# Layer norm of the gathered features with rows on partitions, and the first block row used twice in the ramp: a two-layer graph kernel

## The chip, the cores and the metric

The kernel runs on one core of a Trainium2 chip. Its engines are named as in the profile: PE (TensorE, matmuls; PEld is its weight load), DVE (VectorE), ACT (ScalarE), POOL (GpSimd) and SP (SyncE, which only issues DMAs here). All arithmetic is float32. The metric is the device time of one execution in microseconds (us), less is better. Three runs of the kernel before gave 819.17, 820.83 and 821.37 us, median 820.83.

## The reference

With N = 4096 nodes, D = 128 features and a dense 4096 x 4096 matrix `adj` (64 MB), two layers are computed:

```python
h = relu(adj @ x @ gcn_w + gcn_b)
h = (h - h.mean(-1)) * rsqrt(h.var(-1) + 1e-5) * ln_g + ln_b
xz = h @ w_in                                # 128 -> 2 x 256: xc and z
u = silu(causal_conv4(xc) + conv_b)
dt, B, C = u @ w_xp                          # 8, 16 and 16 columns
dt = softplus(dt @ w_dt + b_dt)
state = exp(dt * A) * state + dt * B * u     # over 4096 steps, 256 x 16 states
y = (sum_s state * C + u * D_skip) * silu(z)
x1 = layernorm(x + y @ w_out)

out1 = MLP3(2 * (adj @ x1)); out2 = MLP3(2 * (adj @ x2))   # eps = 0
out = layernorm(x1 + [out1, out2] @ Wm.T + bm)
```

So `adj` is multiplied three times: with `x`, with `x2` (an input of its own), and with `x1`, which exists only as far as the scan over the nodes has come.

## The kernel before, in words

**Tiling.** `adj` is cut into 8 x 8 blocks of 512 x 512 (1 MB each). Block (n, m) adds, to row chunk n of a product, what the 512 nodes of column m give: 4 matmuls of 128x128 by 128x512 for each product. A block used for `x` and `x2` at once (`ONE`) or for `x2` and `x1` (`DOUBLE`) costs 8 matmuls and one load. `RING = 4` blocks lie in SBUF; SP loads the next one when one is used up. The `x` sums grow in PSUM bank `p_x`, the `x2` sums in `p_x2`; sums for `x1` are made in pieces (`SUMS`) in `p_two`, `p_x` or `p_x2` and added into `acc2` by DVE (`add_sum`, L958).

**Stages.** A *ramp* multiplies block row 0 by `x` (`RAMP`, 32 matmuls), then the chain of steps of chunk 0 runs with matmuls of row 1 between (`FILL`). Then come 8 *chunks* c = 0..7 of 16 *units* (one for each state s), then a tail with the last column of `x1` and the MLPs of layer 2. In unit s of chunk c DVE runs the scan over 512 nodes for the 2 x 128 channels (L933, twice), copies the last state (L941) and multiplies by C (L942); ACT makes exp(dt A) for the next unit into `p_dA` (L687); POOL makes dt B u two units ahead (`times_B`, `bh`, L1116) and adds the product into `y` (`add_product`, L1125). One unit has two *slots* on PE, so a chunk has 32.

**The chain.** Beside the units of chunk c the same engines prepare chunk c + 1 and finish c - 1. Preparing, on PE: `gcn` (L536), `cen` (L539, subtracts the mean by a matmul with a constant matrix), `var` (L542, averages the squares by another), `in_x` (L547, L552), `x_proj` (L565), `dt` (L572). The features lie on the partitions there (`hr` is features x nodes), so the mean over features is a matmul. Between them ACT does relu (L730), square (L734), Ln and Exp (L737, L739) and DVE the product (L976), then the conv taps (L951), `x_sum` (L987) and `dt_sum` (L992). Finishing: POOL multiplies `y` by the gate (`gate_y`, L1137), PE does `out` (L582), DVE adds `x`, takes mean and variance (`bn_stats` L963, `bn_aggr` L969) and negates the means (L1002), and ACT writes `x1` (L809). POOL also makes `dtu` = dt u (L1133). `z` (L557, L559) and the MLP of an `x2` row (L594 to L602; DVE adds the result to `resid` at L1010 or L1012) stand in the same table.

**Order.** Every engine runs its own list in order. `chain_steps` and the two `steps_of` give the unit or slot at which a step stands; `spread_blocks` deals the matmuls of a chunk's blocks over the 32 slots so that each holds about as many matmuls. DVE's list of a unit is: scans, sums that closed in the unit before, steps at place 0, copy and times C, steps at place 1. Semaphores hold a step back until what it reads is there and what it overwrites was read; whatever stands behind it on its engine then waits too.

## Time and profile before

| | us |
|---|---|
| median of three runs | 820.83 |
| the profiled execution, its own time | 821.7 |
| its span in the trace | 819.9 |
| PE busy | 805.8 (98%) |
| POOL busy | 659.7 (80%) |
| DVE busy | 599.7 (73%) |
| ACT busy | 377.9 (46%) |

Shares are averages over the span. DVE and POOL start their main work only with chunk 0, some 70 us in, and have little to do in the tail, so between those points they are busier than the table says. Granted clock is 1.00 in every stretch but the last (0.97), the upper level of 2.4 GHz. A float32 matmul shows as two instructions in the trace, one behind the other, so "x32" there is 16 matmuls. The time between the span and the execution's own time, 1.8 us, lies around the program.

### The profile page before, as it was taken

To read this page: it belongs to the slowest core of one execution; us is meant where nothing else is said; L and a number is where in the kernel's file an instruction comes from. 1 tells how busy PE (TensorE), PEld (TensorE's weight loads), DVE (VectorE), ACT (ScalarE), POOL (GpSimd) and SP (SyncE) were. 2 spreads that over 40 slices of the span, in tenths; PEclk is the share of its full clock that TensorE was granted. 3 is DMA by queue.
4 is the path that set the end of the run, shared out by engine and by line. 5 is a ranking of instruction groups with operands and counts; after the bars stand their busy time and mean duration, and the time that the engine had idled before them with its cause. 6 is when DMAs were issued, how large, how long until landed. Compare 5 with 4: busy or idle time off the path is not lost.

```text
span 819.9 us, 7302 instructions
## 1 busy us (share of the span) xinstructions
PE 805.8 (98%) x2078; PEld 365.8 (45%) x2078; DVE 599.7 (73%) x800; ACT 377.9 (46%) x615; POOL 659.7 (80%) x318
## 2 busy tenths in 40 slices
...
DMA packets 63388, 227.59 MB, mean 278 GB/s; under 512 B 7394, under 2 KB 8052, under 8 KB 44916
## 3 DMA queue, kind: packets, MB, share of 16 engines
...
## 4 chain that ended last, share of the span: by engine, by line
PE 95%; DMA 4%; ACT 1%; DVE 0%; issue 0%; DVEq 0%
PE p_x L486 51%; PE p_x L509 16%; PE p_two L509 11%; DMA x_s<-x_tiles 3%; PE p_m L582 2%; PE p_dA L677 2%; PE p_m L598 2%; PE p_two L572 1%; PE p_m L565 1%; DMA ring<-adj_blocks 1%; PE p_m L602 1%; PE p_m L536 1%; PE p_m L542 1%; PE p_h L677 1%; PE p_m L594 1%; PE p_two L552 1%
## 5 line engine op out<-in xcount | busy, mean ns | idle before, releaser
L486 PE MATMUL p_x<-ring,x_s 128*128 128x512 f32 x1024 | 459.2, 597 | 4.2 <-DMA x_s<-x_tiles 4.2
L1125 POOL TENSOR_TENSOR y<-y,prod 128x1024 f32<-128x1024 f32 x127 | 299.4, 2357 | 26.6 <-DVE prod L942 25.9
L486 PEld LDWEIGHTS p_x<-ring,x_s 128*128 128x128 f32 x1024 | 193.8, 191 | 252.1 <-issue 242.5
L1116 POOL TENSOR_TENSOR bh<-spread,dtu 128x1024 f32<-128x1024 f32 x128 | 302.1, 2360 | 2.1 <-DMA spread<-bc_rows 2.0
L933 DVE TENSOR_TENSOR_SCAN p_h<-p_dA,state,bh 128x512 f32<-128x512 f32 x224 | 276.2, 1279 | 25.3 <-ACT p_dA L687 11.3
L687 ACT ACTIVATE p_dA<-dt,A 128x512 f32<-128x512 f32 x256 | 170.8, 686 | 113.0 <-DVE p_h L933 109.9
L942 DVE TENSOR_TENSOR prod<-p_h,spread_C 128x1024 f32<-128x1024 f32 x128 | 155.3, 1213 | 0.0
L509 PE MATMUL p_x<-ring,x 128*128 128x512 f32 x304 | 137.2, 593 | 0.0
L509 PE MATMUL p_two<-ring,x 128*128 128x512 f32 x208 | 94.5, 593 | 0.5 <-DVE dt L992 0.5
L509 PEld LDWEIGHTS p_x<-ring,x 128*128 128x128 f32 x304 | 57.4, 190 | 72.6 <-issue 72.6
L415 POOL TENSOR_SCALAR dtu<-prod,mv,rstd 128x128 f32<-128x128 f32 x26 | 20.3, 794 | 64.0 <-ACT rstd L920 64.0
L509 PEld LDWEIGHTS p_two<-ring,x 128*128 128x128 f32 x208 | 38.9, 190 | 48.0 <-issue 48.0
L958 DVE TENSOR_TENSOR acc<-p_x,acc 128x512 f32<-128x512 f32 x18 | 12.4, 690 | 49.1 <-PE p_x L509 49.1
L1133 POOL TENSOR_TENSOR dtu<-dt,u 128x1024 f32<-128x1024 f32 x8 | 18.8, 2356 | 35.8 <-DVE dt L992 35.8
L933 DVE TENSOR_TENSOR_SCAN p_h<-p_dA,bh 128x512 f32<-128x512 f32 x32 | 37.5, 1218 | 11.3 <-POOL bh L1116 9.0
L941 DVE COPY state<-p_h 128x2 f32<-128x2 f32 x128 | 19.9, 155 | 15.1 <-DMA spread_C<-bc_rows 4.8
L815 ACT ACTIVATE mb<-p_m,pack 128x512 f32<-128x512 f32 x16 | 11.0, 687 | 36.7 <-PE p_m L598 36.7
L951 DVE SCALAR_TENSOR_TENSOR p_m<-xcv,pack,p_m 128x512 f32<-128x512 f32 x24 | 18.1, 755 | 9.0 <-ACT p_m L754 8.4
L1038 DVE TENSOR_SCALAR u<-pack 128x512 f32<-128x512 f32 x1 | 0.5, 504 | 31.3 <-DMA pack<-pack_w 31.3
L1161 POOL COPY wx<-pack 128x16 f32<-128x16 f32 x1 | 0.2, 197 | 27.4 <-DMA pack<-pack_w 27.4
L760 ACT ACTIVATE gate<-p_m,b_xz 128x512 f32<-128x512 f32 x8 | 5.5, 687 | 32.3 <-PE p_m L557 18.1
L796 ACT ACTIVATE rstd<-mv,eps_t 128x4 f32<-128x4 f32 x8 | 2.4, 297 | 37.5 <-DVE nmean L1002 37.5
...
## 6 DMA issues: line engine op xcount, KB each, us to landing
...
spread<-bc_rows ACTq DMA_DIRECT2D x128, 256.0 KB, 5.1
spread_C<-bc_rows ACTq DMA_DIRECT2D x128, 256.0 KB, 5.7
...
```

The costliest lines, as they stand in the source:

```text
L415: last = eng.tensor_scalar(stage(k)[:, q, :], last_r(k)[:, q, :], mv[:, k % 4, q, 0:1], rstd[:, k % 4, q:q + 1], ALU.subtract, ALU.mult)
L486: return pe.matmul(bank[:, :], tiles[:, JT * m + jt, :], ring[:, i % RING, jt, :], start=opens, stop=closes)
L509: return pe.matmul(sum_bank(no)[:, :], x1[:, m % KEEP, jt, :], ring[:, i % RING, jt, :], start=opens, stop=closes)
L677: pe.matmul(layer_bank(l), W1[:, l, :], moving, start=True, stop=True).then_inc(s_l, 1)
L687: act.activation(p_dA[g][:, :], dt_[:, c % 2, g, :], ACT.Exp, scale=A[:, g, unit:unit + 1]).then_inc(s_dA, 1)
L933: dve.tensor_tensor_scan(p_h[:, g, :], p_dA[g][:, :], bh[:, i % 3, g, :], first, ALU.mult, ALU.add).then_inc(s_scan, 1)
L941: dve.tensor_copy(state[:, unit, :], p_h[:, :, T - 1]).then_inc(s_state, 1)
L942: dve.tensor_tensor(prod[:, i % 2, :, :], p_h[:, :, :], both(spread_C[:, i % SLOTS_C, :]), ALU.mult).then_inc(s_cmul, 1)
L951: dve.scalar_tensor_tensor(out=bank[:, :], in0=xcv[:, g, k:k + T], scalar=conv_w[:, g, k:k + 1], in1=bank[:, :], op0=ALU.mult, op1=ALU.add ...
L1116: pool.tensor_tensor(bh[:, i % 3, :, :], both(spread[:, i % SLOTS, :]), dtu[:, c % 2, :, :], ALU.mult).then_inc(s_bmul, 1)
L1125: pool.tensor_tensor(y[:, c % 2, :, :], y[:, c % 2, :, :], prod[:, i % 2, :, :], ALU.add).then_inc(s_acc, 1)
L1133: pool.tensor_tensor(dtu[:, b, :, :], dt_[:, b, :, :], u[:, :, :], ALU.mult).then_inc(s_dtu, 1)
```

## The change

- **Layer norm of h.** `gcn` becomes four matmuls of 128x128 by 128x128 with the operands swapped, so the result has nodes on partitions. The matmuls `cen` and `var` go. DVE adds the bias and takes relu in two instructions and then mean and variance of each node (`stats`, unit 3), ACT scales and shifts (`norm`, unit 3), DVE transposes 32x32 squares (`turn`, unit 4), and ACT moves the 16 squares to their places in `hr` (`moves`, unit 4; in chunk 0's own preparation ACT and DVE move 8 each). `ln_g` is multiplied into `w_in`, and the matmul that folded the mean into the weights goes.
- **POOL to DVE.** `gate_y` and `dtu` run on DVE (after unit 0's product, and in unit 11). `nmean` is gone: ACT negates `rstd` instead.
- **Earlier steps.** `out` moves from slot 4 to slot 3, `gcn` from slot 7 to 6, DVE's `out` and ACT's `x1` from unit 3 to 2. `z` waits for one MLP result more (`s_res0` n instead of n - 1).
- **Ramp.** Row 0 is multiplied by `x` and `x2` at once: 56 matmuls before the chain and the last 8 among the fill, which has 40 instead of 32. The parts of `x2` are loaded by ACT next to those of `x`. Only block 0 comes in four pieces.
- **Blocks dealt out anew.** `x2` rows are finished in the order 0, 2, 3, 4, 1, 5, 6, 7, an MLP stands in every chunk, and the `x1` sums are cut differently. Loads of blocks: 141 instead of 145.

```diff
--- before.py
+++ after.py
-PIECES = 2
+PIECES = 1
...
+MOVES_0 = 2
...
-RAMP = row(X, 0, ALL)
+RAMP = row(ONE, 0, ALL)
 FILL_BLOCKS = row(X, 1, ALL)
-FILL = {"gcn": 0, "cen": 1, "var": 3, "in_x": 7, "x_proj": 3, "dt": 18}
+FILL = {"gcn": 12, "in_x": 7, "x_proj": 3, "dt": 18}
...
-    row(DOUBLE, 5, ALL[:4]) + row(X2, 5, (5, 6)) + row(DOUBLE, 5, (4,)) + row(X2, 5, (7,))
...
+    row(DOUBLE, 5, (2, 3)) + row(X1, 2, (2, 3)) + row(DOUBLE, 5, (4,)) + row(X2, 6, (6, 7))
...
-X2_ROWS = (2, 3, 4, 0, 1, 5, 6, 7)
-X1_FIRST = (0, 1, 5, 6)
+X2_ROWS = (0, 2, 3, 4, 1, 5, 6, 7)
...
 
-    if c == 0:
-        return []
-    if c < NC - 1:
-        return [(c - 1, (24, 26, 28, 30))]
-    return [(6, (6, 9, 12, 15)), (7, (24, 26, 28, 30))]
+    return [(c, (24, 26, 28, 30))]
...
     if c:
-        put(2, 0, "out", c - 1)
+        put(1, 1, "out", c - 1)
...
-
-        at = tuple(2 * origin(c) + q - (c == 0) for q in (-1, 1, 2, 4, 9, 12))
-        for name, q in zip(("gcn", "cen", "var", "in_x", "x_proj", "dt"), at):
+        at = tuple(2 * origin(c) + q for q in (-2, 4, 9, 12))
+        for name, q in zip(("gcn", "in_x", "x_proj", "dt"), at):
...
-                    pe.wait_ge(s_hr, n + 1)
-                    pe.matmul(p_m[:, :], cen_w[:, :], hr[:, :], start=True, stop=True).then_inc(s_cen, 1)
-                elif name == "var":
-                    pe.wait_ge(s_sq, n + 1)
-                    pe.matmul(p_m[:, :], mean_w[:, :], sq[:, :], start=True, stop=True).then_inc(s_var, 1)
+
+                    for t in range(JT):
+                        last = pe.matmul(p_m4[:, t, :], ax[:, n % 2, P * t:P * (t + 1)], gcn_w, start=True, stop=True)
+                    last.then_inc(s_gcn, 1)
                 elif name == "in_x":
                     pe.wait_ge(s_h, n + 1)
...
-                    block_part(k, 0, JT)
+            for jt in range(JT):
+
+                pe.wait_ge(s_tile[jt], 48 if jt < 2 else 16)
+                block_part(0, jt, jt + 1)
+                block_part(0, JT + jt, JT + jt + 1)
...
+                if name == "norm":
+
+                    act.wait_ge(s_hst, 2 * n + 2)
+                    act.activation(rstd[:, 2 + b, :], mv[:, 2 + b, :, 1], ACT.Ln, bias=eps_t[:, :]).then_inc(s_hrs, 1)
+                    act.wait_ge(s_hrs, 4 * n + 1)
+                    act.activation(rstd[:, 2 + b, :], rstd[:, 2 + b, :], ACT.Exp, scale=-0.5).then_inc(s_hrs, 1)
+                    act.wait_ge(s_hrs, 4 * n + 2)
+                    act.activation(nrstd_h[:, :], rstd[:, 2 + b, :], ACT.Copy, scale=-1.0).then_inc(s_hrs, 1)
+                    act.wait_ge(s_hrs, 4 * n + 3)
+                    for t in range(JT):
+                        last = act.activation(shift_h[:, t:t + 1], mv[:, 2 + b, t, 0:1], ACT.Copy,
+                                              scale=nrstd_h[:, t:t + 1])
+                    last.then_inc(s_hrs, 1)
+                    act.wait_ge(s_hrs, 4 * n + 4)
+                    for t in range(JT):
+                        last = act.activation(sq4[:, t, :], sq4[:, t, :], ACT.Identity,
+                                              bias=shift_h[:, t:t + 1], scale=rstd[:, 2 + b, t:t + 1])
+                    last.then_inc(s_norm, 1)
+                elif name == "moves":
+
+                    act.wait_ge(s_turn, n + 1)
                     wait(act, s_z, G * n)
-                    act.activation(hr[:, :], p_m[:, :], ACT.Relu, bias=w("gcn_b")).then_inc(s_hr, 1)
...
-                elif name == "var":
-                    act.wait_ge(s_var, n + 1)
-                    act.activation(p_m[:, :], p_m[:, :], ACT.Ln, bias=eps_t[:, :]).then_inc(s_ln, 1)
-                    act.wait_ge(s_ln, n + 1)
-                    act.activation(p_m[:, :], p_m[:, :], ACT.Exp, scale=-0.5).then_inc(s_rs, 1)
+                    for q in range(P // Q if n else MOVES_0):
+                        for r in range(P // Q):
+                            last = act.activation(hr4[Q * r:Q * (r + 1), :, Q * q:Q * (q + 1)],
+                                                  turned[Q * q:Q * (q + 1), :, Q * r:Q * (r + 1)], ACT.Copy)
+                    last.then_inc(s_h, 1)
...
-                    put(3, "x1", c - 1)
+                    put(2, "x1", c - 1)
...
-                    put(o - 1, "gcn", c + 1)
-                    put(o, "cen", c + 1)
-                    put(o + 1, "var", c + 1)
+                    put(o - 1, "norm", c + 1)
+                    put(o, "moves", c + 1)
...
+            for jt, tiles in ((0, slice(0, 1)), (1, slice(1, JT))):
+                act.dma_start(x_s[:, tiles, :], x_d[0, :, tiles]).then_inc(s_tile[jt], 16)
+                act.dma_start(x2_s[:, tiles, :], x2_d[0, :, tiles]).then_inc(s_tile[jt], 16)
             for k in range(1, NBLK):
...
-                if name == "var":
-                    dve.wait_ge(s_rs, n + 1)
-                    dve.tensor_tensor(hr[:, :], hr[:, :], p_m[:, :], ALU.mult).then_inc(s_h, 1)
+                if name == "stats":
+                    dve.wait_ge(s_gcn, n + 1)
+
+                    dve.scalar_tensor_tensor(out=sq4, in0=gb_tiles, scalar=-1.0, in1=p_m4,
+                                             op0=ALU.mult, op1=ALU.max).then_inc(s_gb, 1)
+                    dve.wait_ge(s_gb, n + 1)
+                    dve.tensor_tensor(sq4, sq4, gb_tiles, ALU.add).then_inc(s_relu, 1)
+                    dve.wait_ge(s_relu, n + 1)
+                    for t in range(JT):
+                        last = dve.bn_stats(bn6[:, t, :], sq4[:, t, :])
+                    last.then_inc(s_hst, 1)
+                    dve.wait_ge(s_hst, 2 * n + 1)
+                    for t in range(JT):
+                        last = dve.bn_aggr(mv[:, 2 + b, t, :], bn6[:, t, :])
+                    last.then_inc(s_hst, 1)
+                elif name == "turn":
+                    dve.wait_ge(s_norm, n + 1)
+                    wait(dve, s_h, n)
+                    dve.transpose(turned[:, :, :].rearrange("p t n -> p (t n)"), sq[:, :]).then_inc(s_turn, 1)
+                elif name == "moves":
+
+                    dve.wait_ge(s_turn, n + 1)
+                    for q in range(MOVES_0, P // Q):
+                        for r in range(P // Q):
+                            last = dve.tensor_copy(hr4[Q * r:Q * (r + 1), :, Q * q:Q * (q + 1)],
+                                                   turned[Q * q:Q * (q + 1), :, Q * r:Q * (r + 1)])
+                    last.then_inc(s_h0, 1)
...
+                elif name == "dtu":
+                    dve.wait_ge(s_dt, G * (n + 1))
+                    dve.wait_ge(s_u, G * (n + 1))
+                    dve.tensor_tensor(dtu[:, b, :, :], dt_[:, b, :, :], u[:, :, :], ALU.mult).then_inc(s_dtu, 1)
+                elif name == "gate_y":
+                    dve.wait_ge(s_acc, S * (n + 1))
+                    dve.wait_ge(s_gate, n + 1)
+                    dve.tensor_tensor(y[:, b, :, :], y[:, b, :, :], gate[:, :, :], ALU.mult).then_inc(s_yg, 1)
                 elif name == "out":
...
-                    aggregate(s_stats, b).then_inc(s_aggr, 1)
-                    dve.wait_ge(s_aggr, n + 1)
-                    dve.tensor_scalar(nmean[:, :], mv[:, b, :, 0], -1.0, None, ALU.mult).then_inc(s_stats, 1)
+                    aggregate(s_stats, b).then_inc(s_stats, 1)
...
-                    put(3, 0, "out", c - 1)
+                    put(0, 1, "gate_y", c - 1)
+                    put(2, 0, "out", c - 1)
...
-                    put(o + 2, 0, "var", c + 1)
+                    put(o - 1, 0, "stats", c + 1)
+                    put(o, 0, "turn", c + 1)
...
                     put(o + 7, 0, "dt_sum", c + 1)
+                    put(o + 7, 0, "dtu", c + 1)
                 return table
...
-                    pool.wait_ge(s_u, G * (n + 1))
-                    pool.tensor_tensor(dtu[:, b, :, :], dt_[:, b, :, :], u[:, :, :], ALU.mult).then_inc(s_dtu, 1)
-                elif name == "gate_y":
-                    pool.wait_ge(s_acc, S * (n + 1))
-                    pool.wait_ge(s_gate, n + 1)
-                    pool.tensor_tensor(y[:, b, :, :], y[:, b, :, :], gate[:, :, :], ALU.mult).then_inc(s_yg, 1)
-                elif name == "resid":
+                if name == "resid":
                     pool.wait_ge(s_x1, n + 1)
...
-                    if unit == 0 and c:
-                        step("gate_y", c - 1)
-                    if c + 1 < NC and unit == origin(c) + 8:
-                        step("dtu", c + 1)
```

The order of instructions shows what moved. On PE, chunk 0 from its `z` on; `p_x<-ring,x_s` are block matmuls, `ax` is the gathered sum. Before:

```order
L557 MATMUL p_m<-hr,pack 128x512
L559 MATMUL p_two<-hr,pack 128x512
L486 MATMUL p_x<-ring,x_s 128x512 x12
L536 MATMUL p_m<-ax,pack 128x512
L486 MATMUL p_x<-ring,x_s 128x512 x4
L539 MATMUL p_m<-hr,cen_w 128x512
L486 MATMUL p_x<-ring,x_s 128x512 x2
L542 MATMUL p_m<-sq,mean_w 128x512
L486 MATMUL p_x<-ring,x_s 128x512 x5
L547 MATMUL p_m<-hr,pack 128x512
L552 MATMUL p_two<-hr,pack 128x512
```

And now:

```order
L559 MATMUL p_m<-hr,pack 128x512
L561 MATMUL p_two<-hr,pack 128x512
L490 MATMUL p_x<-ring,x_s 128x512 x12
L542 MATMUL p_m<-pack,ax 128x128 x4
L490 MATMUL p_x<-ring,x_s 128x512 x16
L549 MATMUL p_m<-hr,pack 128x512
L554 MATMUL p_two<-hr,pack 128x512
```

Two wide matmuls are gone between `gcn` and `in_x`, and 16 block matmuls stand there in one piece instead of 11 in three.

On DVE, the head of chunk 1 (units 0 to 2; before, `out` follows in unit 3). Before:

```order
L933 SCALAR_TENSOR_TENSOR p_h<-p_dA,state,bh 128x512 x2
L941 COPY state<-p_h 128x2
L942 TENSOR_TENSOR prod<-p_h,spread_C 128x1024
L933 SCALAR_TENSOR_TENSOR p_h<-p_dA,state,bh 128x512 x2
L997 TENSOR_TENSOR dbc<-p_m,x_s 128x512
L963 BN_STATS bn<-dbc 128x6 x4
L969 BN_AGGR mv<-bn 128x2 x4
L1002 TENSOR_SCALAR nmean<-mv 128x4
```

And now:

```order
L1054 TENSOR_TENSOR resid<-p_m,bm 128x512
L945 SCALAR_TENSOR_TENSOR p_h<-p_dA,state,bh 128x512 x2
L953 COPY state<-p_h 128x2
L954 TENSOR_TENSOR prod<-p_h,spread_C 128x1024
L1037 TENSOR_TENSOR y<-y,gate 128x1024
L945 SCALAR_TENSOR_TENSOR p_h<-p_dA,state,bh 128x512 x2
L953 COPY state<-p_h 128x2
L954 TENSOR_TENSOR prod<-p_h,spread_C 128x1024
L945 SCALAR_TENSOR_TENSOR p_h<-p_dA,state,bh 128x512 x2
L1041 TENSOR_TENSOR dbc<-p_m,x_s 128x512
L975 BN_STATS bn<-dbc 128x6 x4
L981 BN_AGGR mv<-bn 128x2 x4
```

The gate product with both inputs in SBUF stands between unit 0 and unit 1, the MLP's result is added ahead of unit 0, and `out` comes one unit sooner without L1002.

On DVE, units 3 and 4 right behind that (before, these hold `out` and nothing else of the chain; `var`, L976, is in unit 6):

```order
L945 SCALAR_TENSOR_TENSOR p_h<-p_dA,state,bh 128x512 x2
L989 SCALAR_TENSOR_TENSOR sq<-gb,p_m 128x512
L992 TENSOR_TENSOR sq<-sq,gb 128x512
L995 BN_STATS bn<-sq 128x6 x4
L999 BN_AGGR mv<-bn 128x2 x4
L953 COPY state<-p_h 128x2
L954 TENSOR_TENSOR prod<-p_h,spread_C 128x1024
L945 SCALAR_TENSOR_TENSOR p_h<-p_dA,state,bh 128x512 x2
L1004 STREAM_TRANSPOSE turned<-sq 128x512
```

Eleven instructions of the layer norm have come into the scan's own queue; one (L976) has left it.

## Rows read from the trace of the kernel before

**Rows 1.** The page: span, and busy time (share) of each engine

```profile
span 819.9 us, 7302 instructions
...
PE 805.8 (98%) x2078; PEld 365.8 (45%) x2078; DVE 599.7 (73%) x800; ACT 377.9 (46%) x615; POOL 659.7 (80%) x318
```

**Rows 2.** What PE waited for, longest first: us in total, times, longest

```profile
PE p_x L486 <- DMA x_s<-x_tiles: 4.2, 3, 1.9
```

**Rows 3.** Timeline of PE, ramp: start, length, [idle before <- releaser]

```profile
4.91 6.66 PE L486 MATMUL p_x<-ring,x_s 128*128 128x512 f32 x8 [1.38 <-DMA x_s<-x_tiles]
...
59.49 0.69 PE L572 MATMUL p_two<-dbc,w_dt 9*128 9x512 f32 x1
```

**Rows 4.** The chain that ended last, in order of time: start, length, what

```profile
60.62 18.22 PE p_x L486 x42
...
415.33 1.78 PE p_m L582 x16
...
750.27 13.73 PE p_x L509 x32
```

**Rows 5.** Timeline of PE, the first matmuls behind chunk 7

```profile
738.02 7.03 PE L509 MATMUL p_x<-ring,x 128*128 128x512 f32 x16
```

**Rows 6.** Timeline of DVE: first scan of chunk 0, then chunk 4

```profile
74.05 2.35 DVE L933 TENSOR_TENSOR_SCAN p_h<-p_dA,bh 128x512 f32<-128x512 f32 x2 [4.89 <-POOL bh L1116]
...
400.78 0.69 DVE L1012 TENSOR_TENSOR resid<-p_m,bm 128x512 f32<-128x512 f32 x1 [4.29 <-PE p_m L602]
...
407.05 2.47 DVE L933 TENSOR_TENSOR_SCAN p_h<-p_dA,state,bh 128x512 f32<-128x512 f32 x2
...
411.03 2.47 DVE L933 TENSOR_TENSOR_SCAN p_h<-p_dA,state,bh 128x512 f32<-128x512 f32 x2
...
438.46 2.34 DVE L951 SCALAR_TENSOR_TENSOR p_m<-xcv,pack,p_m 128x512 f32<-128x512 f32 x3 [0.96 <-ACT p_m L754]
...
483.17 0.69 DVE L1010 TENSOR_TENSOR resid<-p_m,resid 128x512 f32<-128x512 f32 x1 [2.06 <-PE p_m L602]
```

**Rows 7.** What DVE waited for from 400.8 to 483.1 us

```profile
DVE state L941 <- DMA spread_C<-bc_rows: 2.0, 2, 1.0
...
DVE state L941 <- DVE p_h L933: 0.5, 1, 0.5
```

**Rows 8.** DVE by form: busy us, mean ns of one | idle before

```profile
L958 DVE TENSOR_TENSOR acc<-p_x,acc 128x512 f32<-128x512 f32 x18 | 12.4, 690 | 49.1 <-PE p_x L509 49.1
...
L1002 DVE TENSOR_SCALAR nmean<-mv 128x4 f32<-128x4 f32 x8 | 8.0, 1005 | 0.3
...
L963 DVE BATCH_NORM_STATS2 bn<-dbc 128x6 f32<-128x128 f32 x32 | 7.0, 281 | 0.3
...
L969 DVE BATCH_NORM_AGGREGATE mv<-bn 128x2 f32<-128x6 f32 x32 | 3.0, 157 | 0.3
...
L1073 DVE TENSOR_TENSOR y<-y,gate 128x1024 f32<-128x1024 f32 x1 | 1.2, 1225 | 0.0
```

**Rows 9.** Timelines around two instructions of L1002, POOL and DVE

```profile
339.13 0.17 DVE L1002 TENSOR_SCALAR nmean<-mv 128x4 f32<-128x4 f32 x1
...
502.42 2.37 POOL L1116 TENSOR_TENSOR bh<-spread,dtu 128x1024 f32<-128x1024 f32 x1
502.45 2.37 DVE L1002 TENSOR_SCALAR nmean<-mv 128x4 f32<-128x4 f32 x1
```

**Rows 10.** Timeline of POOL, unit 0 of chunk 4

```profile
403.87 2.36 POOL L1137 TENSOR_TENSOR y<-y,gate 128x1024 f32<-128x1024 f32 x1
406.19 2.35 POOL L1116 TENSOR_TENSOR bh<-spread,dtu 128x1024 f32<-128x1024 f32 x1
```

**Rows 11.** ACT by form: busy us, mean ns of one | idle before

```profile
L809 ACT ACTIVATE x<-dbc,shift,rstd 128x128 f32<-128x128 f32 x32 | 13.2, 482 | 0.3
...
L739 ACT ACTIVATE p_m<-p_m 128x512 f32<-128x512 f32 x8 | 4.7, 582 | 0.3
...
L746 ACT ACTIVATE xcv<-xcv 128x6 f32<-128x6 f32 x7 | 1.4, 203 | 0.6 <-issue 0.3
```

155 lines of the change are left out of this document (69 added, 86 removed), and 3 rows, old and new, of the table SUMS.

## The prediction, made before the changed kernel ran

> **What bounds the kernel now.** I read the page first: PE is busy for 805.8 of 819.9 us [rows 1]. Then PE's waits: the largest group is 4.2 us, for parts of `x` in the ramp [rows 2]; nothing behind the ramp comes near it. Granted clock is at the upper level of 2.4 GHz almost throughout, so PE is the bound. A block matmul takes 13.73 / 16 = 0.858 us, `out` 1.78 us for eight narrow ones [rows 4]. The next question is how near the others are. One chunk on DVE runs from the MLP add at 400.78 to the next at 483.17, 82.4 us [rows 6]. In it DVE waits 2.1 us for PE at its end [rows 6] and 7.6 us in six smaller groups [rows 7]: its own work is 72.7 us. POOL takes 2.32 us per instruction back to back [rows 10]; 32 of those, `gate_y`, `dtu` and 1.3 us for `resid` make 80.2 us. So PE leads by only 2 us over POOL and by up to 10 over DVE. That decides this change: it takes 2 us per chunk from PE and 5 from POOL and gives DVE work.
>
> **PE alone.** Each chunk loses `cen` and `var`, 2 x 0.858, and `gcn` becomes 1.78 / 2 = 0.89 instead of 0.86: 1.7 us less, seven times in the chunks and once in the ramp; the folding matmul is another 0.9. The ramp: the first matmul starts at 4.91 [rows 3]; one more DMA of ACT stands ahead (0.4 us), and the third and fourth cost another 0.8 us ahead of the second tile. The 56 matmuls need 48.1 us, and a block of 1 MB with 0.5 MB of `x` and `x2` now feeds 6.9 us of PE, so the waits of [rows 2] go. That gives 54.2; the four narrow `ln_b` matmuls (0.8) hide ACT's copy; then `gcn` 0.9, 12 matmuls 10.3, `in_x` 1.7, 7 matmuls 6.0, `x_proj` 1.2, 3 matmuls 2.6 (77.7), `dt` 1.2, 18 matmuls 15.5: chunk 0 begins at 94.4. Before it began at 60.62 + 18 x 0.858 = 76.1 [rows 4]. Counting the planner's matmuls with these prices, the chunks take 78.9, 80.7, 80.7, 84.1, 77.3, 77.3, 70.4 and 72.2 us, 621.6 in all; before 661.9 (76.1 to 738.0 [rows 5]). PE alone would leave chunk 7 at 716.0 instead of 738.0: 22 us gained, a span of 798.
>
> The chain inside the ramp fits under the 12 matmuls: `stats` 2.6, `norm` 3.4, transpose about 0.7, eight moves 2.0 and semaphores make 9.3 us against 10.3.
>
> **DVE's chunk.** From 72.7 us with two sums. Out: L1002 (0.3 there) and `var` (0.6). In: `gate_y` 1.1 and `dtu` 1.1, by the 1.2 us of L1073 [rows 8] less what overlaps; `stats`, two instructions at 0.71 each, four `bn_stats` at 7.0 / 32 and four `bn_aggr` at 3.0 / 32 [rows 8], less 0.2 us of gap that any step behind a scan fills: 2.5; the transpose, not in this trace, between 0.5 (L739's length on ACT for as many elements) and 1.3 (a scan), taken as 0.6, since nothing in it depends on the element before. Each sum costs 0.45 (0.69 less overlap and that gap). Without sums that is 72.7 - 0.9 - 0.9 + 5.4 = 76.3 us.
>
> **Port waits.** L1002 handles four numbers per partition, from SBUF to SBUF. With POOL idle it takes 0.17 us; at 502.45 it takes 2.37 us and ends with the POOL instruction that began at 502.42 [rows 9]. Two of the eight run with POOL idle; the mean of all is 1.005 us [rows 8], so beside POOL it waits 1.1 us on the mean. No other DVE instruction in the chunks does: each takes at least one input from PSUM, except `bn_stats`, SBUF to SBUF at 281 ns beside POOL. The change adds three per chunk with two SBUF inputs: `gate_y`, the bias add of `stats` (L992) and `dtu`. Each waits between 0 and 2.3 us. I take 1.1 for two, and 2.3 for `gate_y`: it is released by the end of an `add_product`, and POOL starts its next instruction at that moment. That is 4.5 us; below nothing is excluded, as a wait gives nothing back. Behind the waiting instruction stand the scans, for which POOL and ACT wait.
> The Trainium skill (SBUF — State Buffer, "Who interferes with whom") says that a DVE instruction with two SBUF inputs contends with a GpSimd instruction that reads SBUF, and that the second to come waits for the whole of the first. For L1002 the trace agrees; the two-input form beside POOL is in no row here. By that rule it is the forecast, without it the second case below.
>
> Other waits of DVE (parts of C from DMA, `p_dA` while ACT is held by PE) partly stay: 0.8 us. ACT's sixteen moves are cheap: a copy of 6 columns takes 203 ns and one of 512 takes 582 [rows 11], so 128 columns about 0.3, 0.2 apart, 3.3 us in all; they end as DVE ends the next unit. `norm` (four at 482 ns, overlapping) ends under DVE's 3.9 us of product and scan. So K, DVE's chunk without sums, is 76.3 + 4.5 + 0.8 = 81.6 us.
>
> **Who sets the pace.** DVE's chunk starts about 4 us ahead of PE's, because DVE waits for PE's last MLP matmul. `hr` is ready 32 us after that and `u` 47.5 us (37.7 + 6.4 before, [rows 6], plus the new work and waits ahead), while PE reaches `in_x` 30.1, 31.0 and 28.4 and `x_proj` 42.4, 44.9 and 40.6 us into chunks 1 and 2, 3, and 4 and 5. From chunk 4 on PE waits at both; in chunk 6, with only 70.4 us of its own, about 10 us. So DVE is the clock from chunk 1.
>
> Chunk 0: the first scan begins 14.6 us behind the `dt` matmul [rows 3, 6], 1.2 less now, at 91.1. DVE is through scan 3 at 102.7 but `stats` waits for `gcn` of slot 6 (94.4 + 14.6 + 0.9 + 0.3 = 110.2), 7.5 us lost. The rest of the chunk (13 products, 12 scans and the steps) puts the MLP add at 171.4. Six chunks of K = 81.6 make 489.6, their 15 sums 6.8; then PE's chunk 7 with a late `z` and `out`, 73.6, and all behind it as before, 819.9 - 738.0 = 81.9. Sum 823.3. POOL's last products come at 77 us into that stretch and `out` at 80: hidden. The profiled execution is 1.8 us longer than its span and 0.9 above the median, so in terms of the median: 824.
>
> **Rivals.** (a) No port waits: K = 77.1. Then the first chunks are PE's, and waits appear only in chunk 5 (0.5), 6 (6) and at its end (2): 716.0 + 9 + 81.9 = 807, as median 808. For it: `bn_stats` does not wait. Against: L1002. (b) PE keeps the lead throughout, which needs K under about 75: 798, as median 799. It speaks for it that POOL gets 5 us per chunk of room; against, the sum of 76.3. (c) Full waits of 2.3 us three times and a transpose of 1.3: K = 84.7, 842. The other side from the forecast is (a): one mechanism, whether two-input instructions are held by POOL; the point from which it decides is K = 81.0, where the span is the old 819.9. (d) The ramp is not fed (ring and both inputs at once): 5 us on top of any case, unlikely at 1.5 MB per 6.9 us.
>
> **Numbers.** Forecast 824 with 0.53, its own range 815 to 834 (1.5 us of K either way); (a) 0.2, (b) 0.12, (c) 0.12, others 0.03. The range 804 to 835 leaves out most of (b) and the upper part of (c). A difference under 0.3% (2.5 us) can't be told from none. Faster by more: (a), (b) and a tenth of the forecast, 0.37; the same: 0.12; slower: 0.51.
>
> **What would show it.** Right: PE's waits grow from under 8 us to some 30, at `in_x` and `x_proj`, released by ACT's moves and by `u`, in chunks 4 to 6 above all; DVE above 90% between 110 and 640 us; L1037, L992 and L1033 longer beside POOL than alone (means of 3.4, 1.7 and 2.3 us); PE's first chunk at 94; a wait of 7 us of DVE for `gcn` in chunk 0. Wrong: those three at their plain lengths, or PE's waits under 10 us.

## The result: 844.6 us, 3% slower, and the profile after

The changed kernel takes 844.64 us (median of 4 runs, 840.6 to 849.5); the kernel before took 820.12 in the same job (4 runs). The ratio is 1.030 (95% interval 1.025 to 1.034). The direction of the forecast was right, though it had only 0.51 for slower; its size was not: 824 was said, and 844.6 lies outside the range 804 to 835. The profiled execution is the longest of the four (849.5 us, span 847.4), so the sums below are made against 823.3, the span forecast, and not against the median. One run of e3 (851.6 us) and one of e8 (856.4) lie more than 1.5% above the fastest run of the same kernel, may belong to a slower state, and are kept out of the medians below.

The page of the changed kernel, to be held against [rows 1]:

```profile
span 847.4 us, 7586 instructions
...
PE 805.8 (95%) x2092; PEld 367.9 (43%) x2092; DVE 663.3 (78%) x897; ACT 426.7 (50%) x798; POOL 629.8 (74%) x300
...
PE 28%; issue 22%; DVE 21%; POOL 16%; DMA 6%; ACT 5%; ACTq 1%; DVEq 0%; POOLq 0%
```

PE no longer bounds: the chain that ended last, 28% PE here, passes through DVE, POOL and ACT. PE's busy time is as before although its work is 15 us less; most of the reason is the clock: e5 (below), with the same program on PE, is busy for 794.6 us at a mean granted clock of 0.996, the changed kernel for 805.8 at 0.984. What PE waited for (us in total, times, longest), in place of the single group of [rows 2]:

```profile
PE p_m L584 <- ACT gate L770: 7.4, 3, 3.7
PE p_m L549 <- ACT hr L747: 6.7, 5, 4.5
PE p_m L567 <- ACT u L777: 6.3, 5, 1.9
...
PE p_two L554 <- DVE acc L970: 2.9, 1, 2.9
PE p_x L490 <- DMA x_s<-x_tiles: 2.5, 1, 2.5
```

These are `out`, `in_x`, `x_proj`, the second half of `in_x` and the ramp. The window from the MLP add of chunk 0 to that of chunk 6 (window, its length, then busy time of PE, PEld, DVE, ACT and POOL, granted clock, DMA share, GB/s):

```profile
175.00:690.60 515.60, 488.01 (x1260) 221.71 (x1259) 479.42 (x593) 301.41 (x568) 457.89 (x200) 0.98 0.79 277
```

DVE is busy for 479.4 of 515.6 us, 93%, more than POOL with 89%; PE shows 95%, part of it at the lower clock. Six chunks take 515.6 us, 85.9 each, where 496.4 was forecast. The marks of the sum on DVE (start, length; in brackets the idle time and its releaser), for [rows 6]:

```profile
93.92 2.35 DVE L945 TENSOR_TENSOR_SCAN p_h<-p_dA,bh 128x512 f32<-128x512 f32 x2 [2.47 <-POOL bh L1162]
...
113.54 0.69 DVE L989 SCALAR_TENSOR_TENSOR sq<-gb,p_m 128x512 f32<-128x512 f32 x1 [3.58 <-PE p_m L542]
...
175.01 0.68 DVE L1054 TENSOR_TENSOR resid<-p_m,bm 128x512 f32<-128x512 f32 x1
...
690.59 0.68 DVE L1054 TENSOR_TENSOR resid<-p_m,bm 128x512 f32<-128x512 f32 x1
```

The 24.1 us between 847.4 and 823.3 lie so: first scan 93.9 instead of 91.1 (+2.8); from there to the MLP add of chunk 0 81.1 instead of 80.3 (+0.8); six chunks +19.2; behind them 156.8 instead of 155.5 (+1.3).

The new two-input instructions of DVE in that stretch, by form (busy us, mean ns of one, idle before):

```profile
L1037 DVE TENSOR_TENSOR y<-y,gate 128x1024 f32<-128x1024 f32 x7 | 27.0, 3862 | 1.1 <-POOL y L1171 1.1
L1033 DVE TENSOR_TENSOR dtu<-dt,u 128x1024 f32<-128x1024 f32 x6 | 15.0, 2495 | 0.2
...
L992 DVE TENSOR_TENSOR sq<-sq,gb 128x512 f32<-128x512 f32 x6 | 10.0, 1674 | 0.2
...
L1004 DVE STREAM_TRANSPOSE turned<-sq 128x512 f32<-128x512 f32 x6 | 4.1, 688 | 0.0
```

They last 3.9, 2.5 and 1.7 us; alone they take 1.22, 1.22 and 0.69 (measured in the experiments). The mean of `gate_y` hides a surprise. Its first one, and POOL beside it:

```profile
180.64 7.95 DVE L1037 TENSOR_TENSOR y<-y,gate 128x1024 f32<-128x1024 f32 x1 [1.15 <-POOL y L1171]
```

```profile
180.53 2.38 POOL L1162 TENSOR_TENSOR bh<-spread,dtu 128x1024 f32<-128x1024 f32 x1
182.84 2.37 POOL L1171 TENSOR_TENSOR y<-y,prod 128x1024 f32<-128x1024 f32 x1
185.14 2.37 POOL L1162 TENSOR_TENSOR bh<-spread,dtu 128x1024 f32<-128x1024 f32 x1
```

`gate_y` starts 0.11 us behind a POOL instruction and ends 1.1 us behind the end of the third: POOL was not held between its instructions, and DVE got through only when POOL had to wait for DVE's next product. The same happens at 519.9 (7.85 us); the other five take 1.2 to 3.3.

The hold works the other way too, which the forecast did not count: behind the other five, POOL's next instruction (L1171) takes 3.2 to 3.4 us instead of 2.4, as at 270.71.

### The profile page after: what moved, and what is told of

Read it like the earlier page. It is cut to its first block, busy times and chain, and to the rows that moved or that the text cites. A ratio compares the mean times of both kernels' runs of the same rounds, so it can differ in the third digit from the quotient of the medians.

```text
span 847.4 us, 7586 instructions
## 1 busy us (share of the span) xinstructions
PE 805.8 (95%) x2092; PEld 367.9 (43%) x2092; DVE 663.3 (78%) x897; ACT 426.7 (50%) x798; POOL 629.8 (74%) x300
## 3 DMA queue, kind: packets, MB, share of 16 engines
HBM read 220.35 MB, written 2.62 MB: 263 GB/s over the span
## 4 chain that ended last, share of the span: by engine, by line
PE 28%; issue 22%; DVE 21%; POOL 16%; DMA 6%; ACT 5%; ACTq 1%; DVEq 0%; POOLq 0%
POOL y L1171 14%; DVE p_h L945 11%; PE p_x L490 11%; PE p_x L513 6%; PE p_two L513 5%; DVE prod L954 5%; DMA spread<-bc_rows 3%; DMA spread_C<-bc_rows 2%; PE p_dA L673 2%; POOL bh L1162 1%; ACT hr L747 1%; DVE p_two L963 1%; PE p_h L673 1%; DVE p_m L963 1%; ACT p_dA L683 1%
## 5 line engine op out<-in xcount | busy, mean ns | idle before, releaser
L1171 POOL TENSOR_TENSOR y<-y,prod 128x1024 f32<-128x1024 f32 x127 | 304.1, 2395 | 66.7 <-DVE prod L954 66.4
L683 ACT ACTIVATE p_dA<-dt,A 128x512 f32<-128x512 f32 x256 | 173.0, 687 | 161.8 <-DVE p_h L945 157.6
L513 PE MATMUL p_x<-ring,x 128*128 128x512 f32 x288 | 132.4, 602 | 0.0
L513 PE MATMUL p_two<-ring,x 128*128 128x512 f32 x224 | 100.9, 593 | 2.0 <-DVE dt L1028 2.0
L513 PEld LDWEIGHTS p_x<-ring,x 128*128 128x128 f32 x288 | 55.2, 194 | 69.1 <-issue 69.1
L513 PEld LDWEIGHTS p_two<-ring,x 128*128 128x128 f32 x224 | 41.9, 190 | 52.9 <-issue 52.9
L747 ACT ACTIVATE hr<-turned 32x128 f32<-32x128 f32 x120 | 36.9, 307 | 3.0 <-DVE turned L1004 0.7
L1037 DVE TENSOR_TENSOR y<-y,gate 128x1024 f32<-128x1024 f32 x7 | 27.0, 3862 | 1.1 <-POOL y L1171 1.1
L584 PE MATMUL p_m<-pack,y 128*128 128x128 f32 x128 | 19.2, 313 | 7.4 <-ACT gate L770 7.4
L584 PEld LDWEIGHTS p_m<-pack,y 128*128 128x128 f32 x128 | 18.5, 226 | 12.1 <-DVE y L1037 9.8
```

Of the source, the lines that this page charges most:

```text
L513: return pe.matmul(sum_bank(no)[:, :], x1[:, m % KEEP, jt, :], ring[:, i % RING, jt, :], start=opens, stop=closes)
L584: last = pe.matmul(p_m4[:, t, :], y[:, n % 2, g, P * t:P * (t + 1)], w_out[:, g, :], start=g == 0, stop=g == G - 1)
L683: act.activation(p_dA[g][:, :], dt_[:, c % 2, g, :], ACT.Exp, scale=A[:, g, unit:unit + 1]).then_inc(s_dA, 1)
L747: last = act.activation(hr4[Q * r:Q * (r + 1), :, Q * q:Q * (q + 1)], turned[Q * q:Q * (q + 1), :, Q * r:Q * (r + 1)], ACT.Copy)
L1037: dve.tensor_tensor(y[:, b, :, :], y[:, b, :, :], gate[:, :, :], ALU.mult).then_inc(s_yg, 1)
L1171: pool.tensor_tensor(y[:, c % 2, :, :], y[:, c % 2, :, :], prod[:, i % 2, :, :], ALU.add).then_inc(s_acc, 1)
```

## The experiments

Times are medians against the kernel before, which ran beside each of them (820.5 to 821.4).

**DVE beside POOL, measured alone.** m1 computes nothing of the reference. POOL adds SBUF tiles six times back to back; behind the first, DVE issues one instruction at four moments, three times each:

```
for _ in range(6): pool.tensor_tensor(c[i % 4], a, b, ALU.add)
dve.tensor_tensor(o, d, e, ALU.mult)        # and six other forms
```

> A kernel of its own that computes nothing of the reference: POOL adds two SBUF tiles of 128x1024 six times back to back; behind the first of the six DVE issues one instruction (seven forms, at four moments, three times each). Theory 1 (a DVE instruction with two SBUF inputs is held by POOL, and not only by the one that runs): that form takes its own 1.2 us and up to one POOL instruction (2.36 us) more, and in some groups two or three whole ones (4.7 or 7.1 us) more, or until POOL has issued all six; the form with one PSUM input takes 1.2 us always. Theory 2 (it is held by the one running instruction alone, as I forecast): never over 3.6 us; then the two lengths of 7.9 us in the changed kernel have another cause. For the transpose, bn_stats, the copy with one SBUF input and the scan with one PSUM input I expect 0.7, 0.7, up to 1.2 and 1.3 us, no wait.

Lines by form (busy us, mean ns of one, idle before): two inputs from SBUF (L81, L77), one from PSUM (L79), a copy from SBUF to SBUF (L88), scan, transpose and bn_stats with one SBUF input. Then the timeline of the longest one, and POOL in that stretch:

```profile
L81 DVE SCALAR_TENSOR_TENSOR o<-d,e 128x1024 f32<-128x1024 f32 x12 | 36.5, 3038 | 24.6 <-POOL c L55 24.3
L88 DVE COPY o<-e 128x1024 f32<-128x1024 f32 x12 | 30.1, 2507 | 25.1 <-POOL c L55 24.8
L77 DVE TENSOR_TENSOR o<-d,e 128x1024 f32<-128x1024 f32 x12 | 27.2, 2266 | 23.8 <-POOL c L55 23.5
L90 DVE TENSOR_TENSOR_SCAN o<-pm,e 128x512 f32<-128x512 f32 x12 | 14.7, 1224 | 36.8 <-POOL c L55 36.5
L79 DVE TENSOR_TENSOR o<-d,ph 128x1024 f32<-128x1024 f32 x12 | 14.6, 1221 | 36.8 <-POOL c L55 36.5
L84 DVE STREAM_TRANSPOSE o<-e 128x512 f32<-128x512 f32 x12 | 8.5, 711 | 37.9 <-POOL c L55 37.5
L86 DVE BATCH_NORM_STATS2 bn<-e 128x6 f32<-128x512 f32 x12 | 8.3, 695 | 37.4 <-POOL c L55 37.1
```

```profile
354.89 12.53 DVE L81 SCALAR_TENSOR_TENSOR o<-d,e 128x1024 f32<-128x1024 f32 x1 [10.39 <-POOL c L55]
```

```profile
350.22 16.11 POOL L55 TENSOR_TENSOR c<-a,b 128x1024 f32<-128x1024 f32 x7
```

With two SBUF inputs the instruction takes 3.35, 2.62, 1.90 and 1.22 us when it starts 0.07, 0.80, 1.52 and 2.25 us into POOL's running one: apart from the last, which is not held, it ends 3.42 us behind that one's start, whenever it came (17 of the 18 held ones, within 0.01; the other is the long one above). With one input from PSUM it is 1.22 always. Two of the 27 that were held (that at 354.9, and a copy of 12.00 us at 863.1) waited for all five that POOL had left. So the wait is real, and its upper end is not one instruction: theory 1. I had not expected the plain copy to be held; alone it takes 0.70 us, a little over half of the others' time. The Trainium skill (SBUF — State Buffer, "Who interferes with whom") says that two SBUF inputs contend, that a copy can in its two-port modes, and that outside those modes an instruction with one SBUF input does not: the trace agrees. It has the loser wait for the other's whole instruction; 25 of 27 did, two waited for five.

m2 is the same with nine POOL instructions, 48 products and 48 copies, issued 0.07 to 1.3 us into the first (the delay is a PSUM product of 0 to 960 columns).

> A kernel of its own that computes nothing of the reference: POOL adds two SBUF tiles of 128x1024 nine times back to back, and 0 to 1.2 us behind the first DVE issues a product with two SBUF inputs or a copy from SBUF, 48 times each. Theory 1 (the long wait can happen at any contested start, and ends only where POOL pauses): some 5 to 10 of the 96 take 18 to 20 us, until the nine are through, at any phase; the others one POOL instruction at most. Theory 2 (it needs DVE to arrive within 0.1 us of POOL's start, as both long ones of the first port kernel did): long ones only among those issued at once, none among the later.

None of the 96 waited for more than one: products 2.16 to 3.35 us, copies 1.63 to 2.81. Neither theory stands: a start close behind POOL's is not enough. In the kernels it came at starts 0.08 to 1.4 us behind POOL's, in the profiled executions 2 times (changed kernel), 4 (e8), 1 (e9), 1 (e15) and never (e3, e6) of seven. What decides it stays open; always it is three instructions there, until POOL waits for DVE.

**The waits taken out (e1, e2, e3).** e1 gives each of the three one PSUM input, e2 `gate_y` alone (both change the result; a wait of the next scan for their end keeps `p_h` safe, 0.2 us), e3 the bias add alone, with the same result:

```diff
-  dve.tensor_tensor(y[:, b, :, :], y[:, b, :, :], gate[:, :, :], ALU.mult)              # e1, e2
+  dve.tensor_tensor(y[:, b, :, :], y[:, b, :, :], p_h[:, :, :], ALU.mult)
-  dve.tensor_tensor(dtu[:, b, :, :], dt_[:, b, :, :], u[:, :, :], ALU.mult)             # e1
+  dve.tensor_tensor(dtu[:, b, :, :], dt_[:, b, :, :], u[:, :, :] if n == 0 else p_h[:, :, :], ALU.mult)
-  dve.tensor_tensor(sq4, sq4, gb_tiles, ALU.add)                                        # e1, e3
+  dve.tensor_tensor(sq4, p_m4, gb_tiles, ALU.add)
-  dve.scalar_tensor_tensor(out=sq4, in0=gb_tiles, scalar=-1.0, in1=p_m4, ...)           # e3
+  dve.scalar_tensor_tensor(out=p_m4, in0=gb_tiles, scalar=-1.0, in1=p_m4, ...)
```

> The changed kernel in which gate_y, dtu (from chunk 1 on) and the bias add of stats take one of their two inputs from PSUM, as many elements, so that none has two SBUF inputs; the result is not the reference's. Theory 1 (the waits of these three for POOL are what the change costs beyond its work): gate_y, dtu and the add fall from means of 3.9, 2.4 and 1.6 us to 1.25, 1.25 and 0.7, DVE's chunk falls from 85.9 us on the mean of chunks 1 to 6 to about 81, and the time from 844.6 to 812 to 818, where PE bounds again. Theory 2 (DVE is slow by its own work and its gaps; time lost at the three would be lost elsewhere): over 830 us.

> The changed kernel in which gate_y alone takes its second input from PSUM; the result is not the reference's. Theory 1: gate_y is over half of the excess of the three (18 of 34 us in the profiled execution, where two of the seven took 7.9 us): 827 to 833 us, and runs that lie within 3 us of each other instead of 9, because the long waits that come and go are gone. Theory 2: no more than 5 us gained (840 or more), the spread stays.

> The changed kernel with the same result: the maximum of stats is written back to PSUM and the bias add reads it there, so that the add has one SBUF input. Theory 1: the add falls from 1.56 to 0.7 us, 0.9 us in each of seven chunks: 838 to 840. Theory 2: no change (844).

e1: 825.18 us (1.005), e2: 834.60, e3: 834.38 (three runs; 837.08 with the fourth). The three instructions of e1 in the same stretch, and the longest of DVE's waits in chunks 1 to 6:

```profile
L1041 DVE TENSOR_TENSOR y<-y,p_h 128x1024 f32<-128x1024 f32 x7 | 8.5, 1213 | 0.8 <-POOL y L1175 0.7
...
L1037 DVE TENSOR_TENSOR dtu<-dt,p_h 128x1024 f32<-128x1024 f32 x6 | 7.3, 1221 | 0.2
...
L996 DVE TENSOR_TENSOR sq<-p_m,gb 128x512 f32<-128x512 f32 x6 | 4.1, 691 | 0.2
```

```profile
DVE p_h L949 <- POOL bh L1166: 5.1, 5, 1.2
DVE acc L974 <- PE p_two L513: 4.3, 4, 1.2
DVE resid L1058 <- PE p_m L602: 4.3, 3, 2.6
DVE p_h L949 <- ACT p_dA L683: 3.1, 2, 2.7
```

Without the port waits 19.5 of the 24.5 us that the change costs are gone, but e1 missed its 812 to 818: with no port wait left the chunk is still 82.5 us. Its work is 77.5, as forecast (76.3 and 1.1 for the sums); the other 5 us are gaps of up to 2.7 us behind POOL, PE, ACT and DMA. e2 is 1.6 us above its expected 827 to 833, its four runs within 2.3 us of each other. e3 gained 10.3, more than the 4.6 to 6.6 expected; its runs go from 834.4 to 851.6, `gate_y` being untouched. Part of the won time comes back as such gaps: in the profiled executions the port waits were 30 us in six chunks, and without them the listed gaps of DVE grow from 21.7 to 30.2 us.

**The split undone.** e4: `gate_y` back on POOL. e5: `dtu` too. e6: the split alone, put into the kernel before.

```diff
-                    put(0, 1, "gate_y", c - 1)           # e4, e5, DVE's table; + in e6
-                    put(o + 7, 0, "dtu", c + 1)          # e5, DVE's table; + in e6
+                    if unit == 0 and c:                  # e4, e5, POOL's loop; - in e6
+                        step("gate_y", c - 1)
+                    if c + 1 < NC and unit == origin(c) + 8:      # e5; - in e6
+                        step("dtu", c + 1)
```

> The changed kernel with gate_y back on POOL, in its old place behind the product of unit 15; dtu stays on DVE. If gate_y's place on DVE is the main cost (its 1.2 us and its waits of 2.7 us on the mean, three POOL instructions at worst): DVE's chunk falls by 4 us, POOL's rises to about 79, the time is 823 to 829, and no run lies far above the others. If POOL becomes the bound instead: 835 or more.

> The changed kernel with gate_y and dtu both back on POOL: the norm on partitions, the new ramp and the new order stay. DVE's chunk loses 6.5 us against the changed kernel and is 79 to 80; POOL has 33 instructions and resid again, 80.2 us. If the split is what costs: 814 to 822, POOL and PE the bound together. If the norm on partitions costs (its 3.8 us of DVE and the chain over ACT's moves): 828 or more.

> The kernel before with gate_y and dtu moved from POOL to DVE and nothing else. DVE has 72.7 us of work a chunk there; 2.4 and waits of 1.5 to 4 make at most 79.5 under PE's 82.4. Theory 1 (DVE's load decides, the split costs only where DVE is full): 820 to 825. Theory 2 (a held gate_y delays out and PE even where DVE has room): 828 or more.

e4: 834.07 us, between its two cases (823 to 829, and 835 or more), and equal to e2, which takes the wait of `gate_y` away in another way. e5: 831.72 (814 to 822 if the split alone costs; it fell into the other case, 828 or more). e6: 821.56, ratio 1.0005 (0.9992 to 1.0017), no change. The split costs 13 us in the changed kernel and nothing in the one before, where DVE has room and `gate_y` mostly meets an idle POOL: six of its seven take 1.21 us in e6 (POOL's next instruction then takes 3.2 us instead of 2.4, at no cost there). But without it 10 us remain (831.7 against 821.4 beside it). e5 over chunks 1 to 6 (columns as above):

```profile
175.00:670.00 495.00, 476.77 (x1258) 216.12 (x1257) 441.32 (x578) 300.39 (x568) 480.25 (x210) 1.00 0.82 287
```

POOL 97%, PE 96%, DVE 89%. No engine is free to catch up what another loses.

**ACT's moves.** In the changed kernel they stand between DVE's scans like this (ACT, then DVE):

```profile
292.58 4.77 ACT L747 ACTIVATE hr<-turned 32x128 f32<-32x128 f32 x15
...
297.36 0.30 ACT L747 ACTIVATE hr<-turned 32x128 f32<-32x128 f32 x1
...
297.69 0.60 ACT L710 ACTIVATE ax<-p_x 128x512 f32<-128x512 f32 x1
298.31 1.30 ACT L683 ACTIVATE p_dA<-dt,A 128x512 f32<-128x512 f32 x2
```

```profile
293.49 2.47 DVE L945 TENSOR_TENSOR_SCAN p_h<-p_dA,state,bh 128x512 f32<-128x512 f32 x2
...
299.14 2.47 DVE L945 TENSOR_TENSOR_SCAN p_h<-p_dA,state,bh 128x512 f32<-128x512 f32 x2 [1.76 <-ACT p_dA L683]
```

Sixteen take 5.1 us, 0.32 apart, not 3.3; a decay waits behind them and DVE's scan behind it. e8 cuts them in two:

```diff
-                    put(o, "moves", c + 1)
+                    put(o, "moves", c + 1)          # eight
+                    put(o + 1, "moves2", c + 1)     # the other eight, behind the decay of unit 6
```

> The changed kernel, same result, with ACT's sixteen moves of hr cut in two: eight, then the decay of unit 6, then eight. The trace shows the sixteen in 5.1 us and the decay of unit 6 behind them, for which DVE waits 1.1 to 1.8 us in four chunks. If that wait is on DVE's path: 1 us a chunk, 837 to 840. If another (POOL's product, 0.8 to 1.1 us there in the other chunks, or PE, which gets hr 1.4 us later) takes its place: 843 to 846.

e8: 838.03 us (three runs, 834.9 to 842.0; 840.00 with the fourth, 856.4). The profiled one is that fourth, and four of its seven `gate_y` take 6.8 to 8.0 us. In it DVE waits 1.0 us for the decay instead of 4.5, and PE 19 us for `hr` instead of 6.7; how much of this holds for the other three is not known. The gain of 7 us is in the range of the first case (837 to 840), but no larger than the spread of the changed kernel: not settled here.

**The norm undone (e9, e10).** e9 is the changed kernel with the norm by matmuls, e10 the same with both products on POOL: of the change only the ramp, the order and the earlier steps (`out` and `x1`, L1002's negation on ACT) are left.

```diff
-FILL = {"gcn": 12, "in_x": 7, "x_proj": 3, "dt": 18}
+FILL = {"gcn": 4, "cen": 4, "var": 4, "in_x": 7, "x_proj": 3, "dt": 18}
-COST = {"z": 2, "out": 2, "in_x": 2}
+COST = {"z": 2, "out": 2, "in_x": 2, "cen": 0, "var": 0}
# stats, turn (DVE) and norm, moves (ACT) are out; gcn, cen and var are as in the kernel before
```

> The changed kernel with the norm as it was (gcn, cen and var as matmuls with ones, three wide matmuls; no statistics, turn or moves); split, ramp and order stay, and the shares of PE's slots count cen and var as nothing. PE gets 14 us of work back, so PE alone ends at 813 to 815 in the span; DVE's chunk loses 3.9 us of stats and turn with their wait and gets 0.9 of product back. If the norm on partitions is the main cost: 818 to 826. If the split is: 832 or more.

> The same with gate_y and dtu on POOL as before: of the change only the ramp and the new order of blocks, sums, MLPs and out are left. DVE has room again, so PE bounds: 815 to 821. If the earlier out, the earlier MLPs or the ramp cost: 825 or more. Against the kernel with both back on POOL (831.7), the difference is what the norm on partitions costs.

e9: 828.67, between its two cases; e10: 830.10, ratio 1.012 (1.009 to 1.014), where 815 to 821 was expected. This was the finding that the prediction lacked: the ramp and the order, with the earlier steps, cost 9.6 us without the norm and the split. e10 and the kernel before, in a middle stretch and in the late, light chunks:

```profile
98.00:560.00 462.00, 461.76 (x1178) 207.55 (x1177) 390.25 (x476) 245.82 (x399) 444.94 (x195) 1.00 0.82 287
560.00:680.00 120.00, 112.76 (x296) 50.56 (x296) 106.28 (x129) 63.53 (x99) 118.94 (x53) 1.00 0.84 293
```

```profile
560.00:738.00 178.00, 178.00 (x465) 82.03 (x464) 150.05 (x180) 79.87 (x128) 163.65 (x72) 1.00 0.83 295
```

Before, PE never waits there and POOL is 92% busy. In e10 POOL is 99% busy and PE waits 7 us. The new ramp moves the 32 matmuls of row 0 of `x2` ahead of chunk 0. That leaves PE's sum as it is, but DVE and POOL begin their 128 units later (first scan 98.0 instead of 74.05). Up to 560 us PE still never waits in e10, and POOL is 96% busy, as before. Behind that PE has less work in a chunk than POOL's 80.2 us (the forecast counted 70.4 to 77.3 us for the last four, and `cen` and `var` add 1.7), and PE waits. From the first scan to the end e10 takes 729.3 us and the kernel before 745.8: 16.5 won against 23.9 of later start.

**Small mends.** e11 is e4 with e3's edit; e12 is e5 with e3's and e8's edits.

> The changed kernel with gate_y on POOL and the bias add of stats fed from PSUM, same result. If what waits for POOL adds up on DVE: 834.1 less 7 times 0.9, 826 to 829. If DVE's gaps behind the others fill it up: 832 or more.

> The changed kernel with gate_y and dtu on POOL, the bias add fed from PSUM, and ACT's moves cut in two around the decay of unit 6, same result. If the three add up: 831.7 less 6 and less 1 to 6, 820 to 825, as the kernel before. If POOL (80.2 us of work a chunk) is the bound of that version: 829 or more.

e11: 825.59, e12: 822.52 (1.003): 8.5 and 9.2 us better than e4 and e5 (6.3 and 7 to 12 were expected). They add up.

**The old ramp back (e15, e13, e14, e16).** e15 is the changed kernel with ramp, order of blocks, sums and MLPs as before:

```diff
-RAMP = row(ONE, 0, ALL)
+RAMP = row(X, 0, ALL)
-FILL = {"gcn": 12, "in_x": 7, "x_proj": 3, "dt": 18}
+FILL = {"gcn": 11, "in_x": 7, "x_proj": 3, "dt": 11}
 # CHUNK_BLOCKS, SUMS, X2_ROWS, X1_FIRST, mlps and the loads of x and x2 as in the kernel before;
 # so are PIECES, the wait of z, and the negation of the means (nmean) on DVE
```

e13 is e15 with both products on POOL and the edits of e3 and e8; e14 is e13 with `dtu` on DVE; e16 is e13 with the moves in one piece.

> The changed kernel with the ramp and the order of blocks, sums and MLPs as they were (row 0 of x2 in chunks 3 to 5), fills of 11, 7, 3 and 11 matmuls: split, norm on partitions and the earlier out stay. PE has as much work as in the changed kernel. Theory 1 (the longer ramp costs, because DVE and POOL start 17 us later and set the pace from then on): 826 to 832. Theory 2 (the ramp costs nothing or gains, the norm and the split cost all): 842 or more.

> The kernel before with the norm on partitions, the earlier out, the bias add fed from PSUM and the moves cut in two; gate_y and dtu on POOL, ramp and order of blocks as before; same result as the reference. DVE and POOL start at 77 us instead of 94 against the same kernel with the new ramp (822.5), and PE has 14 us less work than before. Theory 1 (POOL and DVE set the pace, so their start counts in full): 806 to 812, faster than both. Theory 2 (start does not count): 820 to 824.

> The same with dtu on DVE instead of POOL: POOL's chunk falls from 80.2 to 77.9 us, DVE's rises by 2.4 with its wait. If POOL is what bounds the one before: 2 to 6 us faster than it. If DVE is: as much slower.

> The kernel with the old ramp, the norm on partitions and both products on POOL (814.8), with ACT's sixteen moves in one piece again, so that hr comes 1.4 us earlier and the decay of unit 6 later. PE waited for hr at in_x 0.8 to 1.4 us in four chunks. If that wait is on the path: 811 to 813. If DVE's wait for the decay takes its place: 814 to 818.

e15: 826.02, as theory 1 said, 18.6 us less than the changed kernel, with the same instructions of the norm and the split, and one instruction of DVE more. In the profiled executions e15 takes 754.1 us from the first scan to the end and the changed kernel 753.5: the whole difference of their spans is that the first scan comes at 72.8 and not at 93.9. e13: 814.82, ratio 0.993 (0.992 to 0.994), faster than both kernels, though 3 us above the expected 806 to 812. PE is 98% busy in it (793.1 of 813.0 us) and leads again; its longest wait is now for `hr`. e14 (814.14) and e16 (815.03, in its second case, 814 to 818) do not differ from it: neither POOL's room nor the moves bound it. The first scans of e15 and e13, and PE's waits in e13:

```profile
72.81 2.35 DVE L942 TENSOR_TENSOR_SCAN p_h<-p_dA,bh 128x512 f32<-128x512 f32 x2 [2.46 <-POOL bh L1161]
```

```profile
73.22 2.35 DVE L945 TENSOR_TENSOR_SCAN p_h<-p_dA,bh 128x512 f32<-128x512 f32 x2 [4.89 <-POOL bh L1154]
```

```profile
PE p_m L551 <- ACT hr L750: 4.9, 6, 1.4
```

All parts of the change together (medians, us; the new ramp and order always with the earlier steps, the old ones in e13 and e15 too):

| | both products on POOL | both on DVE |
|---|---|---|
| old ramp and order, norm by matmuls | 820.5 (before) | 821.6 (e6) |
| old ramp and order, norm on partitions | 814.8 (e13, with the two mends) | 826.0 (e15) |
| new ramp and order, norm by matmuls | 830.1 (e10) | 828.7 (e9) |
| new ramp and order, norm on partitions | 831.7 (e5); 822.5 with the mends (e12) | 844.6 (changed kernel) |

## Why the prediction was wrong in size

**DVE is the clock.** Right in that DVE is 93% busy between 175 and 690 us and that PE waits for what comes from it; but DVE waits for the others as well, as told below. PE's waits are 35 us where 30 were said, but only 16 of them at `in_x` and `x_proj`; the others came at `out`, the MLPs, the sums and the ramp. Of the 28 us that PE is idle between 175 and 690.6, 16 lie in chunks 5 and 6, about where they were forecast.

**DVE's own work.** Right. e1, without port waits, does 77.5 us a chunk; the forecast had 76.3 and 1.1 of sums. (The listed new terms, 1.1, 1.1, 2.5 and 0.6, make 5.3 and not 5.4: 0.6 us in six chunks.) The transpose takes 0.69 us (0.6 was taken), the `bn_` instructions as in [rows 8].

**Port waits, 4.5 us a chunk.** The size was nearly right: in the six chunks (24.2 - 7.4) for `gate_y`, (15.0 - 7.3) for `dtu` and (10.0 - 4.1) for the bias add make 30.4 us, 5.1 a chunk. The step "each waits between 0 and 2.3 us" was wrong: it took one pair of rows [rows 9] for a bound, and two of `gate_y` waited 6.6 and 6.7. It is worth 3.4 of the 19.2 us. The three means forecast (3.4, 1.7 and 2.3 us for `gate_y`, the bias add and `dtu`) came out at 3.9, 1.7 and 2.5.

**"Other waits 0.8" is the step that failed.** What DVE waited for in chunks 1 to 6 (us in total, times, longest):

```profile
DVE p_h L945 <- ACT p_dA L683: 4.5, 4, 1.8
DVE p_h L945 <- POOL bh L1162: 3.4, 3, 1.2
DVE state L953 <- DMA spread_C<-bc_rows: 3.1, 4, 1.3
DVE acc L970 <- PE p_x L513: 2.7, 1, 2.7
DVE acc L970 <- PE p_two L513: 2.6, 4, 1.2
```

With four smaller groups the listed gaps are 21.7 us, 3.6 a chunk, 2.8 more than forecast, 17 us in six. With the 3.4 above and 1 us less of work these are the 19.2. I had 9.7 us of such gaps in a chunk of the kernel before (2.1 in [rows 6] and 7.6 behind [rows 7]), took them for slack that would close once DVE set the pace, and kept 0.8. They closed only in part: 3.6 us a chunk stayed. By what releases them they seem to hang on the order of each engine's program and not on PE's pace: a decay behind sixteen moves of ACT, a product of POOL, a part of C from DMA, a bank that PE has just closed. That reading is argued; the one run made for a single gap (e8) did not settle it. That the gaps stay is shown, best by e1: with the port waits taken away the gaps are 5.0 us a chunk, where rival (a) with its 808 would have had 0.8, and the time is 825.

**Rival (c), 842.** The measured 844.6 lies next to it, and that is luck: it had three full waits of 2.3 us (6.9 us a chunk; 5.1 measured) and a transpose of 1.3 us (0.69 measured), and no more than 0.8 us of other waits.

**ACT's moves, 3.3 us.** They take 5.1. The 0.2 us apart was that of instructions of a few columns, which overlap; these do not. With `take_x` behind them they are the 1.1 to 1.8 us at unit 6 in four chunks. The forecast had nothing for the moves there.

**The ramp.** Chunk 0's `dt` matmul starts at 81.24 and not at 77.7. PE's first matmuls in the ramp:

```profile
6.03 2.93 PE L490 MATMUL p_x<-ring,x_s 128*128 128x512 f32 x3 [2.50 <-DMA x_s<-x_tiles]
```

0.7 us are the first DMAs. The rest is my count: 56 matmuls at 0.858 us, though the first eight passes (two to a matmul) start 0.6 to 1.0 us apart and not 0.43, which [rows 3] had shown (eight in 6.66 us). That the ramp is fed (no wait behind the first) was right. The wait of DVE for `gcn` in chunk 0 is 3.6 us and not 7.5, since DVE came later.

**What the sum did not ask.** I counted the ramp as matmuls moved at no cost and priced "22 us gained" for PE. For DVE and POOL it is 20 us of late start. The forecast contained this number (91.1 instead of 74.05) and I never priced it by itself. e15 and e10 price it together with the order of blocks, sums and MLPs (e10 also with the earlier steps): 18.6 and 9.6 us. No run has the new ramp with the old order; that the start is what counts rests on the equal times behind the first scan in e15 and the changed kernel. Against this, PE alone ending at 798 (rival b) needed a DVE and a POOL with 20 us to spare.

**PE's clock** was not in the forecast. When `gate_y` waited, PE waited for `out`, and its granted clock fell:

```profile
185.00:190.00 5.00, 2.04 (x7) 0.96 (x6) 5.00 (x3) 1.38 (x3) 2.51 (x2) 0.95 0.00 2
190.00:195.00 5.00, 5.00 (x20) 3.90 (x20) 4.78 (x6) 1.92 (x4) 2.53 (x2) 0.71 0.38 113
```

```profile
189.46 3.65 PE L584 MATMUL p_m<-pack,y 128*128 128x128 f32 x16 [2.96 <-ACT gate L770]
```

`out` takes 3.65 us instead of 1.78 [rows 4], as at the lower level of 1.2 GHz, after 3 us without work. What that cost in the span no run separates.
